# Gated convolution block with an 8x8 Fourier filter: the transform applied to the normalized channels before the projection

## The chip, the cores and the metric

One core of one Trainium2 chip runs the whole program. The metric is the device time of one execution in microseconds. TensorE is called PE here, VectorE DVE, ScalarE ACT, GpSimd POOL and SyncE SP, as in the profile.

## What is computed

The input x has 4 images of 32 channels with 128 by 128 pixels. Two layers follow one another; each adds a block of the normalized image to the image:

```python
xm = jnp.einsum('bchw,oc->bohw', x, W_in)                 # 32 -> 3*85 channels, x here normalized
x_spatial, x_freq, x_gate = jnp.split(xm, 3, axis=1)
out_spatial = jax.lax.conv_general_dilated(x_spatial, W_dw, ..., feature_group_count=HID)   # 3x3, per channel
xp = x_freq.reshape(B, HID, h, P, w, P).transpose(0, 1, 2, 4, 3, 5)                         # 8x8 patches
xf = jnp.fft.rfft2(xp)
xf = xf * fft_weight
xi = jnp.fft.irfft2(xf, s=(P, P))
x_fused = jax.nn.gelu(x_gate, approximate=False) * (out_spatial + out_freq)
return jnp.einsum('bchw,oc->bohw', x_fused, W_out)                                          # 85 -> 32
# x = x + block(gn(x)), twice; gn normalizes each channel of each image
```

The projection (over channels) and the Fourier transform (over the pixels of a patch) are both linear and act on different axes, so either can come first.

## The kernel before

The image is cut into Q = 4 bands of 32 columns, and the 128 partitions hold 4 bands x 32 channels. A strip is 8 columns wide in each band (4 strips for an image, 16 for a layer, 32 in all), a tile is 16 rows of a strip (two 8x8 patches, 128 pixels, for all 4 bands at once): 8 tiles to a strip, 256 tiles in both layers. Values are split into a high and a low f16 part (`parts`, HI and LO) and PE multiplies them in f16.

For each strip DVE normalizes into `xn` (L812), ACT rounds to the high part (L544, three shifts), DVE makes the low part (L836, three shifts), and SP copies `parts` into `stack`, where contraction rows are 4 groups of 32 channels (28 DMAs a strip, L273 and L279, two buffers; the buffer of strip s is free when the last tile of strip s-2 has ended, L284).

The main loop is written out by hand as steps, one for each tile, and every engine runs its own list in program order. Step i on PE, in this order: 7 convolution matmuls of tile i for band 0 (`conv`, L395, pixels stationary, 85 columns moving); 4 f32 transposes of the result of tile i-2 (L442); every fourth step, where i mod 4 is 2, the output projection of 4 tiles (L453); 2 gate matmuls and the convolution of band 1; the 4 frequency projections of tile i+3 into `ps_u` (L401); 2 gate matmuls, convolution of band 2; the Fourier transform of tile i+2, three matmuls of 340 columns (`bas` high and low against `uh`, high against `ul`, L482 to L485); convolution of band 3; the inverse transform of tile i, three matmuls of 340 columns (L490 to L493).

Beside it in step i: ACT copies `ft` (L579), rounds `uh` (L585), evaluates the gate's Gelu (L589), rounds `yh` (L594), and in steps 1, 3 and 5 of 8 makes the next strip's high parts. DVE multiplies by the gate (L895), adds the residual every fourth step (L905), in steps 0, 2, 4 and 6 of 8 normalizes and makes low parts, makes `ul` (L925), and multiplies the spectrum by its filter into `y32` (L931). POOL makes the low part `yl` of the filtered spectrum (L654), and seven times in the run sends and gathers statistics by DMAs of its own queue (L616, L622) and moves image edges (L634, L643). `y32`, `yh` and `yl` have two buffers each.

The order at the start is written out too: the first strip is split in two pieces, whose stack loads are shared by SP, POOL and ACT, and SP loads strip 1 after them.

## Time and profile before

| | us |
|---|---|
| median of 3 runs | 830.47 (828.88 to 832.42) |
| the profiled execution, its own time | 829.37 |
| its span | 827.6 |

| engine | busy us | share of the span |
|---|---|---|
| PE | 799.3 | 97% |
| DVE | 612.7 | 74% |
| ACT | 571.5 | 69% |
| POOL | 274.4 | 33% |

The profile is a page with busy shares, the chain of work that ended last and the costliest groups; the trace behind it answers by line, by stretch of time and by engine. A matmul's duration covers its way through the array and overlaps its neighbours': what it costs PE is the difference of the starts of two that follow one another. POOL's and SP's DMA rows are the time to issue; a DMA lands later, and its landing is counted from the start of its issue.

### The profile page before, as it was taken

What the parts mean: (1) busy time and instruction counts of PE and PEld (TensorE: products, weight loads), DVE (VectorE), ACT (ScalarE), POOL (GpSimd) and SP (SyncE); (2) the same over time, 40 slices, a digit from 0 to 9 for tenths busy, and PEclk for the clock granted to TensorE, in tenths of its full rate; (3) what the DMA queues carried; (4) which work ended last, traced back from release to release, by engine and by line L of the source; (5) the groups of instructions that cost most, each with busy time, mean ns of one, the idle gap of its engine ahead of it and who ended that gap; (6) DMA issues with size and microseconds to landing.
All of it is one profiled execution on the core that took longest, in us unless ns stands there. A gap on an engine that the chain in (4) does not pass through costs nothing.

```text
span 827.6 us, 31423 instructions
## 1 busy us (share of the span) xinstructions
PE 799.3 (97%) x12332; PEld 654.8 (79%) x12332; DVE 612.7 (74%) x1153; ACT 571.5 (69%) x1149; POOL 274.4 (33%) x345
## 2 busy tenths in 40 slices
PE   1799999999999999999999999999999999999997
PEld 0588888888888888888888888888888888888885
DVE  7887888888888777687777776667667766767553
ACT  2566676767767777777777777677776777777664
POOL 2724232542336322433234223332232333223221
PEclk9799999999999999999999999999999999999999
DMA  8766557545555445655454665655665655566621
GB/s 295 181 210 145 135 125 211 133 113 128 134 125 140 110 111 118 144 132 130 109 118 114 158 141 142 157 131 134 149 141 146 156 133 134 138 142 156 150 63 51
DMA packets 66522, 115.51 MB, mean 140 GB/s; under 512 B 16242, under 2 KB 18954, under 8 KB 65994
## 3 DMA queue, kind: packets, MB, share of 16 engines
q1 hardware_dynamic: 63606, 110.50, 54.1%
q0 software_dynamic: 2144, 2.59, 1.3%
q8 instruction: 99, 1.62, 0.9%
q10 hardware_dynamic: 628, 0.43, 0.2%
q14 instruction: 45, 0.37, 0.1%
HBM read 10.98 MB, written 8.56 MB: 24 GB/s over the span
## 4 chain that ended last, share of the span: by engine, by line
PE 94%; DVE 3%; issue 1%; DMA 1%; ACT 1%; SPq 0%; POOL 0%; DVEq 0%; ACTq 0%
PE ps_s L395 35%; PE ps_ft L442 15%; PE ps_o L453 8%; PE ps_g L401 6%; PE ps_u L401 5%; PE ps_z L482 5%; PE ps_s L490 5%; PE ps_s L493 4%; PE ps_s L491 4%; PE ps_z L485 4%; PE ps_z L483 4%; DMA x<-in_x 1%; DVE parts L836 1%; DVE st L755 0%; DVE amax L685 0%
## 5 line engine op out<-in xcount | busy, mean ns | idle before, releaser
L395 PE MATMUL ps_s<-cw,stack 128*128 128x85 f16 (+1 forms) x7168 | 457.5, 203 | 0.4 <-DVE f L895 0.4
L395 PEld LDWEIGHTS ps_s<-cw,stack 128*128 128x128 f16 (+1 forms) x7168 | 379.4, 98 | 49.1 <-DVE f L895 0.8
L654 POOL TENSOR_TENSOR yl<-y,yh 128x340 f16<-128x340 f32 x256 | 230.0, 899 | 525.4 <-ACT yh L594 525.4
L594 ACT ACTIVATE yh<-y 128x340 f16<-128x340 f32 x256 | 124.7, 487 | 195.6 <-DVE y L931 124.2
L925 DVE SCALAR_TENSOR_TENSOR ul<-ps_u,uh 128x340 f16<-128x340 f32 x256 | 129.7, 506 | 105.6 <-ACT uh L585 104.7
L836 DVE TENSOR_TENSOR parts<-xn,parts 128x1024 f16<-128x1024 f32 (+2 forms) x99 | 118.1, 1198 | 82.3 <-ACT parts L544 82.0
L579 ACT ACTIVATE ft<-ps_ft 85x512 f32<-85x512 f32 x256 | 149.3, 583 | 20.3 <-PE ps_ft L442 16.7
L442 PE MATMUL ps_ft<-squares_sb,f 128*85 128x128 f32 x1024 | 162.6, 281 | 0.8 <-ACT ft L579 0.8
L895 DVE TENSOR_TENSOR f<-ps_s,g 128x340 f32<-128x340 f32 x256 | 129.4, 505 | 12.5 <-PE ps_s L493 4.0
L589 ACT ACTIVATE g<-ps_g,gsc 128x340 f32<-128x340 f32 x256 | 137.6, 537 | 1.2 <-PE ps_g L401 1.0
L931 DVE TENSOR_TENSOR y<-ps_z,weff 128x340 f32<-128x340 f32 x256 | 128.2, 501 | 1.4 <-PE ps_z L485 1.4
L401 PE MATMUL ps_g<-pw,stack 128*128 128x85 f16 x1024 | 125.2, 205 | 0.0
L585 ACT ACTIVATE uh<-ps_u 128x340 f16<-128x340 f32 x256 | 114.5, 447 | 14.3 <-PE ps_u L401 13.2
L401 PEld LDWEIGHTS ps_g<-pw,stack 128*128 128x128 f16 x1024 | 80.2, 98 | 55.3 <-issue 52.8
L442 PEld LDWEIGHTS ps_ft<-squares_sb,f 128*85 128x85 f32 x1024 | 114.8, 155 | 1.0 <-DVE f L895 1.0
L544 ACT ACTIVATE parts<-xn 128x1024 f16<-128x1024 f32 (+2 forms) x99 | 100.3, 1017 | 15.4 <-DVE xn L820 14.2
L401 PE MATMUL ps_u<-pw,stack 128*128 128x85 f16 x1024 | 81.6, 202 | 1.1 <-DVE weff L732 1.1
L482 PE MATMUL ps_z<-uh,bas 128*128 128x340 f16 x256 | 79.2, 309 | 2.6 <-ACT uh L585 1.7
L490 PE MATMUL ps_s<-yh,inv 128*128 128x340 f16 x256 | 79.0, 309 | 0.0
L485 PE MATMUL ps_z<-ul,bas 128*128 128x340 f16 x256 | 78.7, 308 | 0.1
L493 PE MATMUL ps_s<-yl,inv 128*128 128x340 f16 x256 | 78.5, 307 | 0.0
L483 PE MATMUL ps_z<-uh,bas 128*128 128x340 f16 x256 | 78.5, 307 | 0.0
(96 smaller groups left out, 601.7 us busy)
## 6 DMA issues: line engine op xcount, KB each, us to landing
stack<-parts SPq DMA_DIRECT2D x496, 130.0 KB, 2.5
out_y<-yo SPq DMA_DIRECT2D x16, 512.0 KB, 2.8
stack<-parts SPq DMA_DIRECT2D x124, 65.0 KB, 2.1
stack<-parts SPq DMA_DIRECT2D x124, 64.5 KB, 2.1
stack<-parts SPq DMA_DIRECT2D x124, 64.0 KB, 2.0
x<-in_x SPq DMA_DIRECT2D x3, 2048.0 KB, 10.1
x<-in_x SPq DMA_DIRECT2D x4, 512.0 KB, 5.7
raw<-in_w_raw SPq DMA_DIRECT2D x2, 510.0 KB
```

Source lines behind the costliest of these rows:

```text
L395: mm(ps_s[i % 2][:, HID * q:HID * (q + 1)], pixels(kind, i, q, dy, rows), w[0:rows, m, :], start=(q == 0 and m == 0), stop=False)
L401: t = mm(bank[:, HID * q:HID * (q + 1)], pixels(A, i, q, 0), pw[layer(i)][:, which, :], start=(q == 0), stop=(q == Q - 1))
L442: t = nc.tensor.transpose(ps_ft[0:HID, q * 128:(q + 1) * 128], f[:, k, HID * q:HID * (q + 1)], id32)
L482: mm(ps_z[:, 0:GC], bas[:, 0, :], uh[:, k, :], start=True, stop=False)
L579: nc.scalar.activation(ft[:, (i - 2) % (2 * OUT), :, :].rearrange("p q n -> p (q n)"), ps_ft[0:HID, 0:Q * 128], ACT.Copy).then_inc(s_ft, 1)
L589: nc.scalar.activation(g[:, i % 2, :], ps_g[:, 0:GC], ACT.Gelu, scale=gsc[layer(i)][:, 0:1]).then_inc(s_gelu, 1)
L594: nc.scalar.activation(yh[:, i % 2, :], y32[:, i % 2, :], ACT.Copy).then_inc(s_yh, 1)
L654: nc.gpsimd.tensor_tensor(yl[:, k, :], y32[:, k, :], yh[:, k, :], ALU.subtract).then_inc(s_yl, 1)
L836: v.tensor_tensor(part[:, LO, rows], xn[:, rows, 1 + dx:1 + dx + TW], part[:, HI, rows], ALU.subtract).then_inc(s_xl, 1)
L895: v.tensor_tensor(f[:, k, :], ps_s[k][:, 0:GC], g[:, k, :], ALU.mult).then_inc(s_f, 1)
L925: v.scalar_tensor_tensor(ul[:, k, :], ps_u[k][:, 0:GC], US, uh[:, k, :], ALU.mult, ALU.subtract).then_inc(s_ul, 1)
L931: v.tensor_tensor(y32[:, k, :].rearrange("p (q o) -> p q o", q=Q), ps_z[:, 0:GC].rearrange("p (q o) -> p q o", q=Q), weff[layer(i + 2)][:, ...
```

## The change

The transform moves ahead of the projection. It is now applied to the 32 normalized channels: PE turns the pixels of two tiles (`turn`: the stored `parts`, channels by pixels, times an identity, 4 matmuls of 128 columns into `ps_xt`), ACT copies the turned pixels to `xt` (`turned_over`), PE transforms them one step later (`transform`: 3 matmuls of 128 columns for a tile), ACT and DVE split the spectra of four tiles into `xf` (`hi_of_spectrum`, `lo_of_spectrum`), and POOL's queue copies them into `xs`, where three groups of 32 channels lie on 96 partitions (high, high, low): 12 DMAs of 32 partitions x 512 f16 for four tiles, three in each step, ahead of that step's `yl` in POOL's order. PE then forms `ps_z` by 4 matmuls of 85 columns. `ps_u`, `uh` and `ul` go, and so do the three transform matmuls of 340 columns. The turn of a pair of tiles stands 12 steps before the pair's first tile, the split of a group of four 8 steps before its first tile, its DMAs 6 to 3 steps before, and PE uses it from 2 steps before. The start is reordered and carries the spectra of the first eight tiles; its matmuls that only keep PE busy are split up. Piece 1 of the first strip is loaded by SP and POOL alone. PE waits for both kinds of stack loads at the strip's first convolution, no longer for one kind three steps ahead. Some buffers share memory.

```diff
@@ -38,11 +38,17 @@
 SS = XS * WS
 EPS = 1e-5
 HI, LO = 0, 1
-LEAD = 3
+LEAD = 2
 DRAIN = 4
-WARM = 32
+
+WARM = (6, 4, 8, 4, 6)
 
 OUT = 4
+
+PAIR, GROUP = 2, 4
+PAIRS, GROUPS_OF_TILES = TILES // PAIR, TILES // GROUP
+
+SPECTRA = (0, 0, 1)
 KH = P * (P // 2 + 1)
 
 
...
 THIRDS = [(k, q) for q in range(Q) for k in range(3)]
 
 PIECES = ((0, 72), (72, H))
-FIRST_LOADS = [(PAIRS_HI[0::2], PAIRS_LO[0::2], THIRDS[0::3]), (PAIRS_HI[1::2], PAIRS_LO[1::2], THIRDS[1::3]),
-               ([], [], THIRDS[2::3])]
+FIRST_LOADS = [[(PAIRS_HI[0::2], PAIRS_LO[0::2], THIRDS[0::3]), (PAIRS_HI[1::2], PAIRS_LO[1::2], THIRDS[1::3]),
+                ([], [], THIRDS[2::3])],
+               [(PAIRS_HI[i::2], PAIRS_LO[i::2], THIRDS[i::2]) for i in range(2)]]
 
 
 STATS = [(0, 0), (0, 1), (1, 0), (0, 2), (1, 1), (0, 3), (1, 2), (1, 3)]
...
+
+        xt = sb("xt", [128, PAIR, 2, 128], F16)
+        xf = sb("xf", [128, 2, 2, GROUP * 128], F16)
+        xs = sb("xs", [3 * C, 2, Q, GROUP * 128], F16)
         g = sb("g", [128, 2, GC])
         y32 = sb("y32", [128, 2, GC])
...
@@ -307,12 +325,37 @@
                 for load in hi:
                     if load[0] == k:
                         load_pair(eng, 0, load, loaded[0], a, z)
+            if piece == 0:
+                for q in range(Q):
+                    load_spectrum(eng, 0, q, s_xs_first[0][by], (by,))
             eng.wait_ge(s_xl, before + ORDER.index(1) + 1)
             for load in lo:
                 load_pair(eng, 0, load, loaded[0], a, z)
             eng.wait_ge(s_xl, before + ORDER.index(-1) + 1)
             for load in thirds:
                 load_third(eng, 0, load, loaded[1], a - 2 * TW if a else 0, z - 2 * TW if z < SC else SC)
+
+
+        def turns_at(p):
+            return PAIR * p - 12 if p >= 8 else p - 4
+
+        def leaves_at(h):
+            return turns_at(2 * h + 1) + 2
+
+        def loads_at(h, q):
+            return 4 * h - 6 + q if h > 2 else (3, 3, 4, 4)[q]
+
+        turning = {turns_at(p): p for p in range(4, PAIRS)}
+        transforming = {turns_at(p) + 1: p for p in range(4, PAIRS)}
+        leaving = {leaves_at(h): h for h in range(2, GROUPS_OF_TILES)}
+
+        def load_spectrum(eng, h, q, loaded, rows=range(3)):
+
+            need(eng, s_z, GROUP * (h - 1))
+            for k in rows:
+                eng.wait_ge((s_xfh, s_xfl)[SPECTRA[k]], h + 1)
+                eng.dma_start(xs[C * k:C * k + C, h % 2, q, :],
+                              xf[C * q:C * q + C, h % 2, SPECTRA[k], :]).then_inc(loaded, 16)
 
         def store(sp, strip):
 
@@ -341,6 +384,8 @@
             load_image(1)
             for piece in range(len(PIECES)):
                 load_piece(sp, piece, 0)
+            for q in (0, 1):
+                load_spectrum(sp, 1, q, s_xs_first[1][0])
             for strip in range(1, ALL):
                 load_strip(sp, strip)
...
+            def turn(p):
+
+                strip = PAIR * p // TPS
+                pe.wait_ge(s_xl, (1 if p < 2 else 1 + len(ORDER)) if strip == 0 else splits(strip, 0))
+                need(pe, s_xt, p)
+                for j in range(PAIR):
+                    at = TW + PIX * ((PAIR * p + j) % TPS)
+                    for part in (HI, LO):
+                        col = 128 * (2 * j + part)
+                        m = mm(ps_xt[:, col:col + 128], parts[strip % 2][:, part, 1, at:at + PIX], id16[:, :],
+                               start=True, stop=True)
+                m.then_inc(s_xt_made, 1)
+
+            def transform(p):
+
+                pe.wait_ge(s_xt, p + 1)
+                if p % 2 == 0:
+                    need(pe, s_xfh, p // 2)
+                    need(pe, s_xfl, p // 2)
+                for j in range(PAIR):
+                    out = ps_x[:, 128 * ((PAIR * p + j) % GROUP):128 * ((PAIR * p + j) % GROUP) + 128]
+                    mm(out, xt[:, j, HI, :], bas[:, 0, :], start=True, stop=False)
+                    mm(out, xt[:, j, HI, :], bas[:, 1, :], start=False, stop=False)
+                    m = mm(out, xt[:, j, LO, :], bas[:, 0, :], start=False, stop=True)
+                m.then_inc(s_dft, 1)
+
+            for p in range(4):
+                turn(p)
+                warm(WARM[p])
+                transform(p)
+            warm(WARM[4])
 
...
+            def spectra_loaded(h):
+                if h == 0:
+                    for by in range(3):
+                        pe.wait_ge(s_xs_first[0][by], 16 * Q)
+                elif h == 1:
+                    for by in range(2):
+                        pe.wait_ge(s_xs_first[1][by], 16 * 2 * 3)
+                else:
+                    pe.wait_ge(s_xs[h % 2], 16 * 3 * Q * (h // 2))
...
-                    project(ps_g, 1, i, range(Q // 2))
+                    gate(i, range(Q // 2))
                     if i > 0:
                         conv(i, 1)
-                if live(i, 3):
-                    if begins(i + 3):
-                        stacks_loaded(i + 3, 0)
-                    if (i + 3) % LT == 0:
-                        pe.wait_ge(s_projection, PROJECTIONS * (layer(i + 3) + 1))
-                        pe.wait_ge(s_weff, layer(i + 3) + 1)
-                    need(pe, s_uh, i + 2)
-                    need(pe, s_ul, i + 2)
-                    project(ps_u[(i + 3) % 2], 0, i + 3, range(Q)).then_inc(s_u, 1)
+                if i in turning:
+                    turn(turning[i])
                 if live(i, 0):
-                    project(ps_g, 1, i, range(Q // 2, Q)).then_inc(s_gate, 1)
+                    gate(i, range(Q // 2, Q)).then_inc(s_gate, 1)
                     conv(i, 2)
                 if live(i, 2):
-                    k = i % 2
-                    need(pe, s_uh, i + 3)
+                    if (i + 2) % LT == 0:
+                        pe.wait_ge(s_projection, PROJECTIONS * (layer(i + 2) + 1))
+                        pe.wait_ge(s_weff, layer(i + 2) + 1)
+                    if (i + 2) % GROUP == 0:
+                        spectra_loaded((i + 2) // GROUP)
                     need(pe, s_y, i + 2)
-                    mm(ps_z[:, 0:GC], bas[:, 0, :], uh[:, k, :], start=True, stop=False)
-                    mm(ps_z[:, 0:GC], bas[:, 1, :], uh[:, k, :], start=False, stop=False)
-                    need(pe, s_ul, i + 3)
-                    mm(ps_z[:, 0:GC], bas[:, 0, :], ul[:, k, :], start=False, stop=True).then_inc(s_z, 1)
+                    col = 128 * ((i + 2) % GROUP)
+                    for q in range(Q):
+                        z = mm(ps_z[:, HID * q:HID * (q + 1)], xs[:, (i + 2) // GROUP % 2, q, col:col + 128],
+                               pw[layer(i + 2)][0:3 * C, 0, :], start=(q == 0), stop=(q == Q - 1))
+                    z.then_inc(s_z, 1)
+                if i in transforming:
+                    transform(transforming[i])
                 if live(i, 0):
                     conv(i, 3)
...
+            def turned_over(p):
+
+                act.wait_ge(s_xt_made, p + 1)
+                need(act, s_dft, p)
+                nc.scalar.activation(xt[:, :, :, :].rearrange("p a b n -> p (a b n)"), ps_xt[:, :],
+                                     ACT.Copy).then_inc(s_xt, 1)
+
+            def hi_of_spectrum(h):
+                act.wait_ge(s_dft, 2 * h + 2)
+
+                need(act, s_z, GROUP * (h - 2) + 1)
+                nc.scalar.activation(xf[:, h % 2, 0, :], ps_x[:, :], ACT.Copy, scale=US).then_inc(s_xfh, 1)
+
...
             load_piece(act, 0, 2)
-            load_piece(act, 1, 2)
...
+                if i in leaving:
+                    hi_of_spectrum(leaving[i])
-                if live(i, 3):
-                    k = (i + 3) % 2
-                    need(act, s_u, i + 4)
-                    need(act, s_z, i + 2)
-                    nc.scalar.activation(uh[:, k, :], ps_u[k][:, 0:GC], ACT.Copy, scale=US).then_inc(s_uh, 1)
+                if i in turning:
+                    turned_over(turning[i])
...
             for i in steps():
+                if i in (-1, 0):
+                    load_spectrum(pool, 1, i + 3, s_xs_first[1][1])
+                for h in range((i + 3) // GROUP, (i + 6) // GROUP + 1):
+                    for q in range(Q):
+                        if 2 <= h < GROUPS_OF_TILES and loads_at(h, q) == i:
+                            load_spectrum(pool, h, q, s_xs[h % 2])
...
+                                       ALU.mult, ALU.subtract).then_inc(s_xfl, 1)
 
             v.memset(table[:, :], 0.0).then_inc(s_table, 1)
             v.memset(ones[:, :], 1.0)
...
-                if live(i, 3):
-                    k = (i + 3) % 2
-                    need(dve, s_uh, i + 4)
-                    need(dve, s_z, i + 2)
-                    v.scalar_tensor_tensor(ul[:, k, :], ps_u[k][:, 0:GC], US, uh[:, k, :],
-                                           ALU.mult, ALU.subtract).then_inc(s_ul, 1)
...
+                if i in leaving:
+                    lo_of_spectrum(leaving[i])
```

`bas` and `inv` keep their contents; `id16` is the 128 by 128 identity in f16.

## Rows read from the trace of the kernel before

**Rows 1.** The page: busy time of PE, and its granted clock in 40 slices.

```profile
PE 799.3 (97%) x12332; PEld 654.8 (79%) x12332; DVE 612.7 (74%) x1153; ACT 571.5 (69%) x1149; POOL 274.4 (33%) x345
PEclk9799999999999999999999999999999999999999
```

**Rows 2.** One line of the kernel, L493, the last matmul of a step.

```profile
L493 PE MATMUL ps_s<-yl,inv x256: 306/306/489, 37.6 to 819.8; 128*128 128x340 f16 x128
```

**Rows 3.** Timeline, PE, from step 2 of a strip: start us, us, line, xcount.

```profile
507.69 0.45 PE L395 MATMUL ps_s<-cw,stack 128*128 128x85 f16 x7
507.97 0.63 PE L442 MATMUL ps_ft<-squares_sb,f 128*85 128x128 f32 x4
...
509.91 0.32 PE L401 MATMUL ps_u<-pw,stack 128*128 128x85 f16 x4
510.07 0.24 PE L401 MATMUL ps_g<-pw,stack 128*128 128x85 f16 x2
...
510.43 0.31 PE L482 MATMUL ps_z<-uh,bas 128*128 128x340 f16 x1
...
510.87 0.45 PE L395 MATMUL ps_s<-cw,stack 128*128 128x85 f16 x7
...
511.58 0.45 PE L395 MATMUL ps_s<-cw,stack 128*128 128x85 f16 x7
...
514.38 0.45 PE L395 MATMUL ps_s<-cw,stack 128*128 128x85 f16 x7
```

**Rows 4.** Groups by line: xcount, busy us, mean ns of one, idle before.

```profile
L579 ACT ACTIVATE ft<-ps_ft 85x512 f32<-85x512 f32 x256 | 149.3, 583 | 20.3 <-PE ps_ft L442 16.7
L925 DVE SCALAR_TENSOR_TENSOR ul<-ps_u,uh 128x340 f16<-128x340 f32 x256 | 129.7, 506 | 105.6 <-ACT uh L585 104.7
L905 DVE SCALAR_TENSOR_TENSOR yo<-ps_o,osc,x 128x512 f32<-128x512 f32 x32 | 23.7, 742 | 3.1 <-PE ps_o L453 3.1
```

**Rows 5.** Timeline, POOL, ACT and DVE, around steps 4 and 5 of the strip.

```profile
515.27 0.83 POOL L654 TENSOR_TENSOR yl<-y,yh 128x340 f16<-128x340 f32 x1 [1.96 <-ACT yh L594]
518.90 0.83 POOL L654 TENSOR_TENSOR yl<-y,yh 128x340 f16<-128x340 f32 x1 [2.80 <-ACT yh L594]
...
515.03 1.04 ACT L544 ACTIVATE parts<-xn 128x1024 f16<-128x1024 f32 x1
518.27 0.49 ACT L594 ACTIVATE yh<-y 128x340 f16<-128x340 f32 x1 [0.95 <-DVE y L931]
...
516.17 1.23 DVE L836 TENSOR_TENSOR parts<-xn,parts 128x1024 f16<-128x1024 f32 x1 [1.09 <-ACT parts L544]
```

**Rows 6.** Lines L279, L622 and L643, POOL's DMAs: ns, then us to landing.

```profile
L279 POOL DMA_DIRECT2D stack<-parts x8: 496/500/515, 21.9 to 29.9; - x8
DMA to landing us min/median/max: 2.6/3.4/4.3
...
L622 POOL DMA_DIRECT2D gathered<-sums x28: 548/552/597, 68.8 to 450.0; - x28
...
DMA to landing us min/median/max: 1.9/2.3/4.0
...
DMA to landing us min/median/max: 1.7/2.1/3.9
```

**Rows 7.** Timeline, DVE and POOL, where a normalization meets `yl` in step 0.

```profile
502.73 0.94 DVE L812 TENSOR_SCALAR xn<-x,mv,rstd 128x1280 f32<-128x1280 f32 x1
502.99 1.38 POOL L654 TENSOR_TENSOR yl<-y,yh 128x340 f16<-128x340 f32 x1 [1.86 <-ACT yh L594]
```

**Rows 8.** Timeline, SP's queue and PE: strip 1 at the start, a later strip.

```profile
44.64 7.87 SPq L279 DMA_DIRECT2D stack<-parts  x12
...
60.23 0.45 PE L395 MATMUL ps_s<-cw,stack 128*128 128x85 f16 x7
...
379.57 11.68 SPq L273 DMA_DIRECT2D stack<-parts  x16
391.31 8.47 SPq L279 DMA_DIRECT2D stack<-parts  x12
```

More of the change, by code:

```diff
@@ L211, in build @@
                    for i in range(len(PIECES))]
-        s_u = sem("s_u")
-        s_uh = sem("s_uh")
-        s_ul = sem("s_ul")
+        s_id16 = sem("s_id16")
+        s_xt_made = sem("s_xt_made")
+        s_xt = sem("s_xt")
+        s_dft = sem("s_dft")
+        s_xfh = sem("s_xfh")
+        s_xfl = sem("s_xfl")
+        s_xs_first = [[sem(f"s_xs_first_{by}_{h}") for by in ("sp", "pool", "act")] for h in range(2)]
+        s_xs = [sem(f"s_xs{i}") for i in range(2)]
         s_z = sem("s_z")
@@ L250, in staged @@
         def staged(i, parts_of_a_strip):
-            if i < 0:
-                at = 2 * (i + LEAD)
-                return 1, [p for p in parts_of_a_strip.values() if at <= p < at + 2 or i == -1 and p > at]
             strip, at = i // TPS + 2, i % TPS
@@ L296, in load_strip, with count @@
                 load_third(eng, strip, load, s_stk[strip % 2][1])
+        def count(loads, kind):
+            return 16 * (len(loads[0] + loads[1]), len(loads[2]))[kind]
         def load_piece(eng, piece, by):
-            (hi, lo, thirds), loaded = FIRST_LOADS[by], s_first[piece][by]
+            (hi, lo, thirds), loaded = FIRST_LOADS[piece][by], s_first[piece][by]
             first, last = PIECES[piece]
@@ L396, in conv, with gate @@
                        start=(q == 0 and m == 0), stop=False)
-            def project(bank, which, i, bands):
+            def gate(i, bands):
                 for q in bands:
-                    t = mm(bank[:, HID * q:HID * (q + 1)], pixels(A, i, q, 0), pw[layer(i)][:, which, :],
+                    t = mm(ps_g[:, HID * q:HID * (q + 1)], pixels(A, i, q, 0), pw[layer(i)][:, 1, :],
                            start=(q == 0), stop=(q == Q - 1))
                 return t
+            def spectra_loaded(h):
[7 more added lines that the diff above has]
+                    pe.wait_ge(s_xs[h % 2], 16 * 3 * Q * (h // 2))
             def stacks_loaded(tile, kind):
-                def count(loads):
-                    return 16 * (len(loads[0] + loads[1]), len(loads[2]))[kind]
                 strip = tile // TPS
                 if strip == 0:
-                    for by, loads in enumerate(FIRST_LOADS):
-                        need(pe, s_first[tile // (TPS // 2)][by][kind], count(loads))
+                    for by, loads in enumerate(FIRST_LOADS[tile // (TPS // 2)]):
+                        need(pe, s_first[tile // (TPS // 2)][by][kind], count(loads, kind))
                 else:
-                    pe.wait_ge(s_stk[strip % 2][kind], (strip + 1) // 2 * count((PAIRS_HI, PAIRS_LO, THIRDS)))
+                    pe.wait_ge(s_stk[strip % 2][kind], (strip + 1) // 2 * count((PAIRS_HI, PAIRS_LO, THIRDS), kind))
             def begins(tile):
@@ L422, in conv_begins @@
                 if begins(i):
+                    stacks_loaded(i, 0)
                     stacks_loaded(i, 1)
@@ L552, in hi_part @@
                     need(act, s_s, (strip - 2) * TPS + 1)
+                    if strip == 2:
+                        for by, loads in enumerate(FIRST_LOADS[1]):
+                            for kind in range(2):
+                                act.wait_ge(s_first[1][by][kind], count(loads, kind))
                 hi(strip, dx, slice(0, H))
-            def hi_piece(piece):
-                act.wait_ge(s_xn, 2 * piece + 2)
-                for dx in ORDER:
-                    hi(0, dx, slice(*PIECES[piece]))
             act.wait_ge(s_table, 1)
@@ L737, in first_taps @@
                 dve.wait_ge(s_vl, 1)
-                for kind in (A, BB):
-                    for k in range(4):
-                        _, dx, part = GROUPS[k][kind]
-                        v.tensor_copy(cw[0][C * k:C * k + C, 3 * kind:3 * kind + 3, :],
-                                      (vh, vl)[part][C * k:C * k + C, dx + 1::3, :]).then_inc(s_taps, 1)
+                for part, groups in ((vh, slice(0, 3 * C)), (vl, slice(C, 2 * C))):
+                    last = v.tensor_copy(cw[0][groups, 0:6, :].rearrange("p (k t) o -> p k t o", k=2),
+                                         part[groups, :, :].rearrange("p (t d) o -> p d t o", d=3)[:, 1:3, :, :])
+                    if part is vh:
+                        link(last)
+                last.then_inc(s_taps, 6)
             def image_stats(b, n):
```

103 lines of the change are left out of this document (66 added, 37 removed).

## The prediction

> **What bounds the kernel now.** I read the page's busy shares first: PE 97%, no other engine above 74%, at a granted clock of 9 tenths or more in all slices but one [rows 1]. That makes PE the candidate, and the rest is asked of it. The last matmul of a step stands at 37.6 us for the first tile and at 819.8 for the last [rows 2]: 782.2 us for 255 steps, 3.067 each, 24.5 for a strip of eight. The timeline of one strip, read by differences of starts, says what fills them: a plain step takes 2.80 us (511.58 to 514.38) and the step with the output projection 3.89 (507.69 to 511.58), so four take 3 x 2.79 + 3.89 = 12.27, which is 4 x 3.067: every step of the run is like these, PE is never late, and a matmul removed is time removed as long as nothing takes its place. Seven convolution matmuls of 85 columns cost 0.28, 40 ns each; the four frequency projections 510.07 - 509.91 = 0.16; the three transform matmuls of 340 columns 510.87 - 510.43 = 0.44, 147 ns each [rows 3].
>
> **PE's own sum.** Removed for a tile: 0.16 + 0.44 = 0.60 us. Added: four matmuls of 85 columns for `ps_z`, 4 x 0.040 = 0.16; two of 128 columns to turn, three of 128 to transform. No row shows an f16 matmul of 128 columns. Scaled by columns from 340 it is 0.147 x 128 / 340 = 55 ns, from 85 it is 0.040 x 128 / 85 = 61; its bounds are the 40 of an 85-column one below and the 147 of a 340-column one above. I take 55, since the larger size carries less of the cost of starting: 5 x 0.055 = 0.275. Added 0.435, net 0.60 - 0.435 = 0.165 us a tile, 0.66 for four. With 61 it is 0.135. After the start 248 steps are left: 248 x 0.165 = 40.9 us (33.5 with 61 ns).
>
> A new even step is then 2.79 - 0.60 + 0.16 + 0.22 (the turn of two tiles) = 2.57 and an odd one 2.79 - 0.60 + 0.16 + 0.33 (their transform) = 2.68, the one with the projection 3.67; a strip is 23.2.
>
> **DVE and ACT.** DVE loses `ul`, 0.51 a tile, and gains the low part of four tiles' spectra; the nearest row is 512 elements out of PSUM, 0.74, or 0.19 a tile. ACT loses `uh`, by columns 0.58 x 340 / 512 = 0.39 a tile or a little more, and gains a copy of 512 elements for two tiles and one for four, at 0.58 each: 0.44 [rows 4]. Both had room for this (74% and 69%), so these cost nothing by themselves, covered by PE; without the cover ACT's order counts, in step 4 of a strip (below).
>
> **POOL.** It gains three DMA issues in each step, ahead of `yl`. The nearest row for one of 32 partitions x 1 KB is its own stack load, 0.50; a gather takes 0.55 [rows 6]. 3 x 0.50 + 0.83 = 2.33 us of a mean step of 2.90: it fits, in the time in which POOL waited for `yh` (1.96 and 2.80 us in the rows) [rows 5]. What is queued behind the issues is `yl`, for which the filtering of two tiles later and the inverse transform wait, some 3 us after its usual end. The gathers (4 x 0.55, seven times) may use that up: under 1 us each, in the range, not in the sum.
>
> **The new wait, where I expect part of the gain to go.** PE's `ps_z` of the first tile of a group, in a step whose number is 2 mod 4, waits for DMAs of which the last three are issued in the step before. Call T the start of a step. `yl` starts 515.27 - 514.38 = 0.89 after T [rows 3, 5]. In step 1 of a strip: in step 0 `yl` meets the normalization and takes 1.38 [rows 7], to T0 + 2.26; three issues end at T0 + 3.8, which is T1 + 1.2, the next `yl` at 2.06, and the third issue after it starts at T1 + 3.1. PE wants `ps_z` in step 2 at 2.74 - 0.16 + 0.22 = 2.80, which is T1 + 5.48: 2.4 us are allowed for the landing. In step 5: step 3's high part on ACT (515.03 before) now has the split of a spectrum, the copy of `ft`, the Gelu and the turned pixels behind it before the next `yh`, some 0.95 + 4 x 0.47 after 515.03; that is 517.9 where it was 518.27 (there it waited for `y32` behind the low part of 516.17 and `ul`), `yl` follows 0.63 later and ends at 519.3, in the new count T5 + 2.4; the third issue starts at T5 + 3.4 and 2.1 are allowed. Against this the landings from start of issue: gathers 1.9 / 2.3 / 4.0, edges 1.7 / 2.1 / 3.9, stack loads in the crowded start 2.6 / 3.4 / 4.3 (least, median, most) [rows 6]. The gathers are nearest (24 KB, at the same steps of a strip, while SP loads a stack), so 2.3: step 1's groups are in time and step 5's 0.2 late; the long landings add, by my estimate, 0.17 to either. Mean 0.27 us for each of 62 groups, 17 us. Bounds: 0 with 1.9, and 1.2 us, 74 in all, with 3.4.
>
> **The start.** SP is busy with stack loads without a gap; strip 1's last issue ends at 44.64 + 7.87 = 52.5, lands 2.1 later by the edges' median, and step 8 starts at 60.2, so 5.6 us of slack [rows 6, 8]. SP gains 4 issues for the first spectra, 2 more thirds and 6 for the second: 12 x 7.87 / 12 = 7.9 us, past the slack by 2.3. I put 2.3 us there, between -1 and 4; the earlier first steps are worth nothing, as PE then stands before step 8.
>
> **SP afterwards.** A strip's 28 issues take 11.68 + 8.47 = 20.2 us, with the landing 22.3 [rows 8], of 24.5 before and 23.2 now. Cost nothing, with about 0.9 us of cover.
>
> **Sum.** 829.4 (profiled run, its span 827.6 and 1.8 around it) + 2.3 - 40.9 + 17 = 807.8. The median before stands 1.1 above its profiled run: 809.
>
> **Rivals.**
> 1. The spectra land in time and the gain comes whole: 829.4 + 2.3 - 40.9 + 1.1 = 792. For it, the least landings; against it, that step 5 allows only 2.1.
> 2. Slower: the landings of the last three spectrum DMAs are as in the start, 3.4 us. Then each group waits 1.2 us: 792 + 74 = 866. It decides at (40.9 - 2.3) / 62 = 0.62 us late for each group, a landing of some 2.85. For it, the rows of the same kind of transfer, SBUF to SBUF beside SP's loads; against it, that those were queued behind each other.
> 3. Just around that point, 0.55 to 0.8 us late: 826 to 842.
> 4. SP's loads of a strip, now beside 14% more traffic (384 packets of 1 KB in four tiles), stretch from 20.2 to 23, and with the landing outlast the 23.2: 2 us for each of 31 strips, 62 in all, 854 at worst, 823 if it is half of that. Against it: the issues set the pace, not the landings.
> 5. The 128-column matmul costs about 80 ns, between the 61 and the 147: 0.60 - 0.16 - 0.40 = 0.04 a tile, 10 us in all, and with the wait of the forecast 829.4 + 2.3 - 10 + 17 + 1.1 = 840; as steps are longer then, the wait shrinks, 823 to 840. Against it: weights are loaded for each 85-column matmul within its 40 ns. The Trainium skill states such a price (TensorE: Matmul & The Clock Gate, Back-to-back issue gap): a sustained stream at 128 columns with a weight load each runs at about 81 ns a matmul. The trace doesn't agree in its neighbourhood (40 ns at 85 columns, 147 at 340), and so this has a small chance.
> 6. POOL's DMA issue is held while a normalization runs. `yl` is: 1.38 us in place of 0.83 beside L812, once a strip [rows 7]. If the three issues after it lose as much, step 1's groups are 0.5 later, 31 x 0.5 = 16 us: 825. The Trainium skill has this rule (SBUF — State Buffer, Who interferes with whom): a DMA of GpSimd's queue needs that engine to write descriptors over the port pair that VectorE's two-port modes lock, and SP's or ACT's queue should be used instead. The trace agrees for `yl`; no POOL DMA here met a normalization in the loop.
>
> **How the numbers follow.** Forecast (0.1 to 0.45 us late, 797 to 819, rival 6's milder half in it) 0.45; rival 1, 0.20; rival 6 in full and rival 3 together, 0.12 (a third of it faster, half the same, the rest slower); rival 2, 0.10; rival 4, 0.07 (half same, half slower); rival 5, 0.06 (half faster, a third the same). The band of 0.5% is about what a measurement can tell from no change, 826.3 to 834.6. Faster 0.45 + 0.20 + 0.04 + 0.03 = 0.72; same 0.06 + 0.03 + 0.02 = 0.11; slower 0.17. Range: from 788 (rival 1 with 53 ns) to 836; above it lie rival 2 and the worst of 3, 4 and 5, about 0.17. Within the forecast itself 797 to 819.
>
> **What would show it.** Right: differences of starts of 0.22 for `turn`, 0.33 for `transform`, 0.16 for `ps_z`; PE idle before `ps_z` in steps 2 mod 4 alone, released by DMA into `xs`, longer in steps 6 than in steps 2 of a strip; POOL's issues at 0.50 and its busy time near 650 us; steps 2.57 and 2.68; step 8 starting near 62. Wrong: idle of PE before `ps_s` for `yl` (then POOL is too full), before the first convolution of a strip (then SP), a step of four longer than 11.6 without idle (then the matmul's price), or POOL issues over 0.6 us.

## The result, and the profile after

The changed kernel takes 874.97 us (median of 4 runs, 872.05 to 879.0) against 829.67 for the one before (4 runs beside it): 1.054 times as long, interval 1.049 to 1.060. The forecast was 809, its range 788 to 836, so it is wrong in sign and outside its range. The profiled execution took 879.0 us, its span 877.2: 49.6 us more than the profiled run of before.

The page of the changed kernel: busy times, the clock granted to PE in 40 slices, the chain that ended last, and three of its groups (line, operation, xcount, busy us, mean ns, idle before and its releaser). They answer to [rows 1, 4].

```profile
PE 790.4 (90%) x12840; PEld 672.1 (77%) x12840; DVE 559.1 (64%) x956; ACT 573.0 (65%) x1087; POOL 643.5 (73%) x1101
...
PEclk9698999899999999999999989999999999899999
...
PE 47%; POOL 19%; DMA 15%; issue 8%; ACT 6%; DVE 3%; ACTq 1%; POOLq 0%; SPq 0%; DVEq 0%
...
L357 POOL DMA_DIRECT2D xs<-xf x754 | 377.2, 505 | 11.9 <-issue 9.5
...
L567 PE MATMUL ps_z<-pw,xs 96*128 96x85 f16 x1024 | 83.4, 206 | 51.1 <-DMA xs<-xf 50.6
...
L654 ACT ACTIVATE xt<-ps_xt 128x512 f16<-128x512 f32 x128 | 75.4, 589 | 8.6 <-issue 4.8
```

PE has lost its 97%: it is busy for 9 us less and stands still. One wait is new and large, the one before `ps_z` for the spectra. The chain, which before was PE's, now runs through POOL and the DMAs.

The first question is whether PE's own work became shorter, as planned. The timeline of an undisturbed odd and an even step (start us, us, line, xcount) answers to [rows 3]:

```profile
560.57 0.45 PE L474 MATMUL ps_s<-cw,stack 128*128 128x85 f16 x7
...
562.05 0.31 PE L567 MATMUL ps_z<-pw,xs 96*128 96x85 f16 x4
562.20 0.22 PE L454 MATMUL ps_x<-bas,xt 128*128 128x128 f16 x1
...
562.54 0.45 PE L474 MATMUL ps_s<-cw,stack 128*128 128x85 f16 x7
...
563.25 0.45 PE L474 MATMUL ps_s<-cw,stack 128*128 128x85 f16 x7
...
564.38 0.39 PE L442 MATMUL ps_xt<-id,parts 128*128 128x128 f16 x4
564.60 0.24 PE L480 MATMUL ps_g<-pw,stack 128*128 128x85 f16 x2
...
565.84 0.45 PE L474 MATMUL ps_s<-cw,stack 128*128 128x85 f16 x7
```

Differences of starts: the odd step 563.25 - 560.57 = 2.68, the even one 2.59, the transform of two tiles 562.54 - 562.20 = 0.34, the turn 0.22, `ps_z` 0.15. These are the forecast's 2.68, 2.57, 0.33, 0.22 and 0.16. A strip without a wait takes 23.3 us by these steps (24.53 before); experiment 3 shows it. Where no turn or transform is left, in the last 12 steps, a plain step takes 2.36. Together that is the 41 us that PE's sum promised.

So 829.4 - 41 = 788, and 91 us came on top. The last matmul of each of the 256 steps, first and last of them (it answers to [rows 2]), and the first convolution of step 8:

```profile
L579 PE MATMUL ps_s<-yl,inv x256: 306/306/492, 43.2 to 869.4; 128*128 128x340 f16 x128
...
69.90 0.45 PE L474 MATMUL ps_s<-cw,stack 128*128 128x85 f16 x7 [1.01 <-DVE f L1024]
```

Step 8 starts at 69.90 where it was 60.23 [rows 8]: 9.7 us. Read from the starts of these matmuls, the 31 groups whose `ps_z` stands in step 2 of a strip are late by 51 us together (1.64 each), the 31 in step 6 by 12 (0.39 each). The other steps take 18 us more than their length, 16 of them the steps right behind ten of these waits. 788 + 9.7 + 63 + 18 = 879.

**Where the wait comes from.** All landings of POOL's spectrum DMAs, then those of the last three DMAs of two groups of one strip, issued in its step 1 and in its step 5, and the share of the 16 DMA engines over that strip (576 to 600 us in 40 slices):

```profile
L357 POOL DMA_DIRECT2D xs<-xf x754: 496/498/1091, 23.1 to 853.8; - x189
...
DMA to landing us min/median/max: 1.7/2.3/9.2
```

```profile
L357 POOL DMA_DIRECT2D xs<-xf x3: 496/496/512, 580.4 to 581.4; - x3
...
DMA to landing us min/median/max: 3.0/3.1/3.1
...
L357 POOL DMA_DIRECT2D xs<-xf x3: 496/496/512, 593.0 to 594.0; - x3
...
DMA to landing us min/median/max: 1.9/1.9/2.0
```

```profile
DMA  4263659989899887965979965540445674656697
```

The median of all, 2.3, is just what I had assumed, and it misleads. A landing depends on the step of the strip in which the DMA is issued: by median 2.0, 2.9, 3.0, 2.5, 2.1, 2.0, 1.9 and 1.7 us in steps 0 to 7. Steps 1 to 3 are those in which SP's large pair loads are under way (the nines of the last row). Step 1 had been given the longer allowance, 2.4 us, and needs 3.2 for the last DMA of its group.

The 51 us of the step 2 groups divide so, by issue and landing of each group's last DMA. Twenty-one groups issued on time (by median 2.9 us after the start of step 1) wait 13.6 us together. Four behind a gather of statistics (last issue 4.4 to 5.8 after it) wait 15.6. Two beside a 2 MB image load (landings 8.4 and 6.0) wait 10.9. Two wait 5.6, where POOL stood 2.15 and 1.94 us in the midst of the group's issues with nothing to wait for that the trace shows, and two, issued 3.7 after it behind an edge copy, wait 5.0. So a quarter of the 51 us is the usual landing, and three quarters are rare events. The step 6 groups are as forecast: last issue 3.3 us after the start of step 5, landing 2.2.

**The clock behind a wait.** Timeline and stretches of the group behind a gather (columns of the stretches: busy us and count by engine, PE's granted clock, DMA share, GB/s):

```profile
505.65 1.53 POOL L357 DMA_DIRECT2D xs<-xf  x3
508.12 0.47 PE L567 MATMUL ps_z<-pw,xs 96*128 96x85 f16 x4 [3.94 <-DMA xs<-xf]
508.39 0.71 PE L474 MATMUL ps_s<-cw,stack 128*128 128x85 f16 x7
```

```profile
499.00:503.20 4.20, 4.20 (x65) 3.05 (x64) 3.19 (x7) 3.20 (x6) 4.17 (x8) 1.00 0.92 231
504.40:508.10 3.70, 0.00 (x0) 0.00 (x0) 0.00 (x0) 0.57 (x2) 2.78 (x5) 0.81 0.84 222
508.10:512.40 4.30, 4.28 (x43) 3.81 (x44) 2.02 (x5) 1.28 (x3) 1.72 (x3) 0.50 0.57 156
```

Before the wait POOL is busy for 4.17 of 4.20 us: it works off the gather's backlog, and the group's loads leave late. In the wait PE does nothing, and its granted clock falls from 1.00 to a mean of 0.81. After it PE runs for some 4 us at a granted clock of 0.50, the lower of its two levels (1.2 GHz of 2.4); seven convolutions show 0.71 us instead of 0.45. Short waits mostly have no such price: the 21 groups issued on time are late by at most 1.9 us, and the steps behind all of them together take 0.1 us more than their length; the ten others are late by 2.2 to 6.8 us, and the steps behind them take 16 more. Between the two it goes either way: PE stands idle 1.7 us before `ps_z` in step 50 and as long in step 58, and only in step 50 does its granted clock fall to 0.50. (Of the 51 us, 4 are slow matmuls too: `ps_z` itself starts 47 us late in these steps, the rest follows it within the step.)

**The start.** The queues of ACT and SP:

```profile
24.44 2.52 ACTq L357 DMA_DIRECT2D xs<-xf  x4
27.06 2.50 ACTq L293 DMA_DIRECT2D stack<-parts  x4
29.66 0.60 ACT L654 ACTIVATE xt<-ps_xt 128x512 f16<-128x512 f32 x1 [4.78 <-issue]
...
26.71 2.50 SPq L293 DMA_DIRECT2D stack<-parts  x4
33.14 6.00 SPq L287 DMA_DIRECT2D stack<-parts  x8
```

ACT issues eight DMAs from 24.4 to 29.6, and its high parts of piece 1 stand behind them (32.5); SP, which needs these, idles from 29.2 to 33.1. The forecast had counted SP's added issues and taken SP to stay busy.

### The profile page after: what moved, and what is told of

Same layout as the page of the kernel before. It is cut to its first block, busy times and chain, and to the rows that moved or that the text cites. A ratio compares the mean times of both kernels' runs of the same rounds, so it can differ in the third digit from the quotient of the medians.

```text
span 877.2 us, 32629 instructions
## 1 busy us (share of the span) xinstructions
PE 790.4 (90%) x12840; PEld 672.1 (77%) x12840; DVE 559.1 (64%) x956; ACT 573.0 (65%) x1087; POOL 643.5 (73%) x1101
## 4 chain that ended last, share of the span: by engine, by line
PE 47%; POOL 19%; DMA 15%; issue 8%; ACT 6%; DVE 3%; ACTq 1%; POOLq 0%; SPq 0%; DVEq 0%
PE ps_s L474 18%; DMA xs<-xf 14%; POOL xs L357 9%; POOL yl L772 8%; PE ps_ft L529 7%; PE ps_z L567 4%; PE ps_s L576 3%; PE ps_s L579 3%; PE ps_s L577 3%; PE ps_g L480 3%; PE ps_o L540 3%; ACT yh L703 2%; ACT turned_results L691 1%; PE ps_xt L442 1%; ACT xt L654 1%
## 5 line engine op out<-in xcount | busy, mean ns | idle before, releaser
L357 POOL DMA_DIRECT2D xs<-xf x754 | 377.2, 505 | 11.9 <-issue 9.5
L955 DVE TENSOR_TENSOR parts<-xn,parts 128x1024 f16<-128x1024 f32 (+2 forms) x99 | 124.7, 1261 | 93.9 <-ACT parts L630 93.7
L529 PE MATMUL ps_ft<-squares_sb,f 128*85 128x128 f32 x1024 | 167.5, 287 | 0.8 <-ACT turned_results L691 0.8
L691 ACT ACTIVATE turned_results<-ps_ft 85x512 f32<-85x512 f32 x256 | 149.4, 584 | 28.5 <-PE ps_ft L529 28.2
L567 PE MATMUL ps_z<-pw,xs 96*128 96x85 f16 x1024 | 83.4, 206 | 51.1 <-DMA xs<-xf 50.6
L529 PEld LDWEIGHTS ps_ft<-squares_sb,f 128*85 128x85 f32 x1024 | 118.7, 159 | 1.0 <-DVE f L1024 1.0
L567 PEld LDWEIGHTS ps_z<-pw,xs 96*128 96x128 f16 x1024 | 55.3, 100 | 57.7 <-DMA xs<-xf 56.5
L654 ACT ACTIVATE xt<-ps_xt 128x512 f16<-128x512 f32 x128 | 75.4, 589 | 8.6 <-issue 4.8
L576 PE MATMUL ps_s<-yh,inv 128*128 128x340 f16 x256 | 80.9, 316 | 0.0
L577 PE MATMUL ps_s<-yh,inv 128*128 128x340 f16 x256 | 80.0, 313 | 0.0
L540 PE MATMUL ps_o<-turned_results,wo 85*32 85x512 f32 x512 | 68.2, 605 | 0.7 <-ACT turned_results L691 0.7
```

The lines of the kernel that those rows point to most:

```text
L357: eng.dma_start(xs[C * k:C * k + C, h % 2, q, :], xf[C * q:C * q + C, h % 2, SPECTRA[k], :]).then_inc(loaded, 16)
L529: t = nc.tensor.transpose(ps_ft[0:HID, q * 128:(q + 1) * 128], f[:, k, HID * q:HID * (q + 1)], id32)
L567: z = mm(ps_z[:, HID * q:HID * (q + 1)], xs[:, (i + 2) // GROUP % 2, q, col:col + 128], pw[layer(i + 2)][0:3 * C, 0, :], start=(q == 0), s ...
L691: nc.scalar.activation(ft[:, (i - 2) % (2 * OUT), :, :].rearrange("p q n -> p (q n)"), ps_ft[0:HID, 0:Q * 128], ACT.Copy).then_inc(s_ft, 1)
L955: v.tensor_tensor(part[:, LO, rows], xn[:, rows, 1 + dx:1 + dx + TW], part[:, HI, rows], ALU.subtract).then_inc(s_xl, 1)
```

## Experiments

The theory after the result, A: PE's saving is real, and the loss is lateness of the spectra, which makes the transfers' time before `ps_z` the only thing to repair. The rival, B: the work that the change adds (754 issues on POOL, traffic beside SP's loads, POOL's time) slows other things, and would do so if nobody waited for the spectra.

**1. The loads a step earlier.**

```diff
-            return 4 * h - 6 + q if h > 2 else (3, 3, 4, 4)[q]
+            return 4 * h - 7 + q if h > 2 else (3, 3, 4, 4)[q]
```

> The changed kernel with POOL's spectrum loads one step earlier (steps 7 to 4 before a group's first tile in place of 6 to 3), nothing else moved. Theory A, late landing: what the change lost in its loop is PE's wait for these DMAs before ps_z (63 us in the profile of after, in steps 2 and 6 of a strip) and the halved clock behind the long ones (14 us). A step is 2.7 us, and only waits longer than that are left, some 11 us: 875 - 52 - 11 = about 812. Theory B, crowding: the 12% of DMA time and the 377 us of POOL's issues slow the rest wherever they stand: 870 to 880.

Measured 824.11 us (5 runs, 821.19 to 827.18), 0.993 of before (0.990 to 0.996): 51 us less than the change as made, by one number. The waits of this kernel (us, times, longest):

```profile
PE ps_z L567 <- DMA xs<-xf: 12.0, 8, 3.0
```

A holds in direction; its 812 was missed by 12.

**2. The spectra not read.** The loads are issued as before, but `ps_z` multiplies a constant in place of `xs`, so the Fourier branch of the result is left out, and PE doesn't wait for them in the loop. ACT and POOL wait instead, before they use a buffer again, until the loads out of it have landed; that costs ACT 1.4 us and PE nothing that its waits show.

```diff
-                    z = mm(ps_z[:, HID * q:HID * (q + 1)], xs[:, (i + 2) // GROUP % 2, q, col:col + 128],
+                    z = mm(ps_z[:, HID * q:HID * (q + 1)], bas[0:3 * C, 0, :],
```

> The changed kernel, but from tile 8 on ps_z is formed from the constant basis and not from the spectra: the result is not the reference's. All loads are still issued at their places and land, PE waits for none. Theory A: the loop runs at its own steps, 2.58, 2.69 and 3.68 us: about 797 (start as in after, to 72.3; 29 strips of 23.27; the rest 50). Theory B: 840 or more.

Measured 817.69 us (2 runs). Neither 797 nor 840: 57 us of the loss is the wait for the spectra with its consequences, and some 15 to 20 (this run against experiment 3 and against the 797 expected) is B's. The waits name it:

```profile
PE ps_s L579 <- POOL yl L776: 10.8, 7, 3.2
```

In the strips with gathers POOL is a step behind, and `yl` is late as well.

**3. No loads in the loop.** As 2, with POOL's issues in the loop left out too.

```diff
-                            load_spectrum(pool, h, q, s_xs[h % 2])
+                            pass
```

> As the run whose spectra are not read, and POOL's spectrum loads of the loop left out too (the result is not the reference's; turn, transform and splits are all still done). Theory A: the same as that run within 4 us, about 797 or a little less, since issues and traffic by themselves cost nothing. Theory B: under 800 here and 40 us or more between the two runs.

Measured 802.18 us (2 runs), 0.966 of before. From strip 2 to the last but two a strip takes 23.3 us, but for two of 23.8 and 23.5; strip 1 takes 25.9. The run lies 15.5 below experiment 2, not within 4 as A had it: the loads cost that much even where nobody reads them. Issues and transfers went out together here, so their shares aren't separated; the 10.8 us for `yl` in experiment 2 point to the issues. It is the floor for anything done to the loads alone: PE's 41 us are there, the start's 9.7 are not repaired.

**4. The kernel before, with the loads.** Three DMAs of 32 partitions x 1 KB in each step, from a table that lies ready, which nobody reads and nobody waits for.

```diff
+                if 2 <= i < 246:
+                    q = (i - 2) % 4
+                    need(pool, s_spare[q], 16 * 3 * ((i - 2) // 4))
+                    for k in range(3):
+                        pool.dma_start(ft_all[96:128, ...], squares_sb[C * q:C * q + C, :, :]...).then_inc(s_spare[q], 16)
```

> The kernel before, with three extra DMAs of 32 partitions x 1 KB issued by POOL ahead of yl in each of steps 2 to 245, from a constant into memory nobody reads: the change's traffic and issues alone. Theory A: 830 within 3 us, with SP's landings longer but nobody late. Theory B: 850 to 875.

Measured 838.84 us (2 runs), 1.010 of before (1.006 to 1.015). Its line and one wait that it has and before has not:

```profile
L657 POOL DMA_DIRECT2D ft<-squares_sb x732: 496/498/1092, 43.5 to 799.3; - x183
...
DMA to landing us min/median/max: 1.7/2.5/9.0
...
PE ps_u L403 <- DMA stack<-parts: 3.6, 2, 2.4
```

This kernel measures what was disputed, the landing, without the change: by median 2.3, 2.7, 3.1, 3.0, 2.3, 2.0, 2.0 and 1.7 us for issues in steps 0 to 7 of a strip, the same course, with 9.0 at worst beside an image load. So the long landings don't come from how `xf` is made. In both kernels they fall in the steps of SP's pair loads (0.87 to 1.01 of the DMA engines' time in steps 1 to 3, 0.2 to 0.3 in step 7); that these loads are the cause is inferred from this, as no run moved or left out the burst. The loads by themselves cost 9 us here, in the steps beside gathers and image loads (step 37, beside image 3's, takes 5.39 instead of 2.79).

**5. The gathers on ACT's queue.** Sends, gathers and edges move from POOL's list to ACT's, the four gathers of a lot spread over three steps, the rest as changed.

```diff
+            def gather(e, q):
+                act.wait_ge(s_sent, 16 * e)
+                act.wait_ge(s_mv, e)
+                act.dma_start(gathered[C * q:C * q + C, :, :], sums[e].rearrange("(q c) n -> c q n", q=Q)).then_inc(s_gathered, 16)
```

> The changed kernel with the statistics' sends and gathers and the edge transfers issued by ACT's queue (gathers spread over three steps) in place of POOL's, which leaves POOL the spectrum loads, yl and small work; the loads stand where the change has them. If POOL's backlog after a gather is what made the last loads late by 4 to 6 us in the groups of steps 42, 74, 106 and 138 (15.6 us of wait there, and 7 of slow clock behind it), those are gone and the landing beside the pair loads stays: 875 - 20 = 855, within 8. If the backlog matters little: 870 or more. If ACT becomes late by it: PE would idle before its gate matmuls.

Measured 866.09 us (2 runs).

```profile
PE ps_z L567 <- DMA xs<-xf: 49.4, 42, 5.0
```

In the groups of step 2 the late issues are gone (last issue 2.9 by median, 3.7 at most, and the mean falls from 1.64 to 1.34 us late), but the groups of step 6 rose from 0.39 to 0.63. Of the 20 us expected 9 came. What took the rest stands in POOL's timeline:

```profile
201.32 0.50 POOL L357 DMA_DIRECT2D xs<-xf  x1 [2.49 <-issue]
...
325.33 0.50 POOL L357 DMA_DIRECT2D xs<-xf  x1 [2.50 <-issue]
```

Six times POOL stands 2.5 us before a DMA issue with no releaser in the trace, exactly 120 of its DMAs apart, and each time in step 5, among the last loads of the group of step 46, 86, 126, 166, 206 or 246. These six steps take 8.9 us more than their length.

**6. Both.** Experiments 1 and 5 together.

> Both: spectrum loads a step earlier, and sends, gathers and edges by ACT. The run with early loads alone was at 824, with PE still waiting in the strips with a gather (steps 10, 42, 74, 106, 138) and where an image is loaded. Theory A with the backlog: some 15 us less, 808 to 812. If the rest is due to traffic alone: 822 to 826.

Measured 814.92 us (4 runs, 812.81 to 817.15), 0.982 of before (0.979 to 0.985): 9 less than experiment 1, with the ranges apart. POOL's six pauses are there as in experiment 5, but the earlier loads cover them: the steps behind them are at their length.

```profile
PE ps_z L567 <- DMA xs<-xf: 4.7, 2, 2.8
```

```profile
L357 POOL DMA_DIRECT2D xs<-xf x7: 496/496/514, 149.8 to 159.5; - x7
...
DMA to landing us min/median/max: 5.6/7.6/7.9
```

From step 48 on the strips are at 23.3 to 24.1 us up to the last steps, which are so short that PE waits 2.1 for the last strip's stack. The rest of what is left sits beside the image loads: the second fence is the stretch of image 3's, where spectra land after 5.6 to 7.9 us.

**7. A pause of PE, by itself.** In the kernel before, PE waits in step 2 of 31 strips for twelve memsets of POOL.

```diff
+                if i % TPS == 2 and 10 <= i < TILES:
+                    pool.wait_ge(s_s, i)
+                    for n in range(PAUSE):
+                        nc.gpsimd.memset(spare[:, :], 0.0).then_inc(s_pause, 1)
...
+                    if i % TPS == 2 and i >= 10:
+                        pe.wait_ge(s_pause, PAUSE * (i // TPS))
```

> The kernel before, with PE waiting before ps_z in step 2 of each strip from step 10 on (31 times) for 12 chained memsets of POOL, no other change. It measures what an idle time of about 3 us costs beyond itself. If the granted clock falls behind such a wait, as the profile of after shows behind waits over 2 us, 830 + 31 x (the wait + 1 to 2 us); if that was an effect of the traffic, 830 + 31 x the wait, and the next steps stay at 2.79.

Measured 1027.66 us (2 runs), span 1024.9, 197.3 more than before.

```profile
PE ps_z L487 <- POOL spare L658: 114.6, 31, 6.7
```

```profile
416.00:419.00 3.00, 2.81 (x21) 2.04 (x22) 0.92 (x2) 0.35 (x1) 0.05 (x1) 0.50 0.54 125
...
422.00:424.00 2.00, 2.00 (x36) 1.80 (x34) 1.02 (x2) 0.98 (x2) 0.35 (x1) 1.00 0.43 100
```

The waits make 114.6 us, 3.7 each; the other 82.7, 2.7 for each wait, lie behind them, where PE works at a granted clock of 0.50 (2.81 us busy for 21 matmuls) until it is back at 1.00. A wait of 3.7 us costs 6.4. The forecast's sum had priced a microsecond late at a microsecond.

**8. The order of the start.** ACT makes the high parts of piece 1 before its eight DMA issues, DVE the low parts before the loop.

```diff
+            hi(0, ORDER[1], slice(*PIECES[1]))
+            hi(0, ORDER[2], slice(*PIECES[1]))
             load_piece(act, 0, 2)
             turned_over(2)
```

> The changed kernel with one edit in the start: ACT makes the high parts of piece 1 before its 8 DMA issues (which hold it for 5.1 us) and DVE its low parts before the loop. SP was idle from 29.2 to 33.1 us waiting for them and its loads of strip 1 set when step 8 starts (68.7 against 60.2 before). Expected: step 8 about 4 us earlier, total 871 within 3. If the first steps are bound by the turn and its copies instead: 875 again.

```profile
29.20 5.15 SPq L287 DMA_DIRECT2D stack<-parts  x8
...
66.68 0.45 PE L474 MATMUL ps_s<-cw,stack 128*128 128x85 f16 x7
...
PE ps_z L567 <- DMA xs<-xf: 60.2, 46, 5.5
```

SP's piece 1 leaves at 29.20 instead of 33.14 and step 8 starts at 66.68 instead of 69.90. Yet it measures 881.5 us (2 runs, 879.86 to 883.14), 6.5 more than the change as made: the waits before `ps_z` are 60.2 us here against 50.6. Why they grew, this run doesn't tell.

**9. Image loads in quarters.** Experiment 6, with images 2 and 3 loaded by four DMAs of 0.5 MB each, image 2's one behind the stack loads of strip 1 and three between those of strip 2, image 3's one for a strip.

```diff
-                    load_image(2)
-                if strip == 4:
-                    load_image(3)
+                    quarter(2, 0)
+                if strip in (3, 4, 5, 6):
+                    quarter(3, strip - 3)
```

> The kernel of e6 (POOL's loads of the spectra a step earlier, gathers, sends and edges issued by ACT), in which the loads of images 2 and 3, 2 MB each, are four loads of 0.5 MB: image 2's in the strip loads of strips 1 and 2, image 3's one behind each of the strip loads 3 to 6. What is left of e6 over its own nominal strip are steps 9, 10 and 11 (+5.3 us together) and steps 33 and 34 (+4.4 us), both beside an image load. Theory A (a 2 MB load keeps the 16 engines for some 6 us, and spectra issued meanwhile land after 7 to 9 us): steps 33 and 34 back to 2.69 and 3.7, steps 9 to 11 back by half or more, 807 to 809 us. Rival B (the same bytes cost the same time wherever they stand, spread over more steps): 813 to 816.

Measured 810.79 us (4 runs), 0.977 of before (0.975 to 0.979). Steps 34 and 35, which the text on record counts as 33 and 34, are back at their length (3.68 and 2.69 from 7.28 and 3.54), as A had it. Image 2 went wrong: steps 14 and 15 take 7.33 and 6.79.

```profile
DVE mv L932 <- DMA gathered<-sums: 8.5, 1, 8.5
```

Three quarters between the pair loads hold everything behind them (median landings of 8 to 11 us by kind of DMA, the gathers among them), and DVE waits for these in its order with the filter and the gate behind it.

**10. With the order of the start.**

> The kernel of e9, and the order of e8 in the start: ACT's high parts of piece 1 before its own eight DMA issues, DVE's low parts of that piece before the loop. In e8 step 8 began 3 us earlier (65.8 against 68.7) and the waits before ps_z ate it. Theory A (those waits were late spectra, which the earlier loads have removed): the 3 us stay, 804 to 806 us. Rival B (the early strips are held by SP's loads of the first strips, whose order is not changed): within 1 us of e9.

Measured 808.19 us (4 runs, 803.89 to 812.62), 0.973 of before (0.970 to 0.976). Steps 10 and 11 are undisturbed now, 14 and 15 (7.62 and 6.75; its next text counts them as 13 and 14) are not. The runs of 9 and 10 overlap, so the gain of the start isn't shown by their medians. (Its text puts step 8 of two kernels at 65.8 and 68.7; the first convolutions stand at 66.68 and 69.90.)

**11. Image 2 behind strip 2.** Experiment 10, with the last three quarters of image 2 behind strip 2's stack loads.

```diff
+                if strip == 2:
+                    for n in (1, 2, 3):
+                        quarter(2, n)
```

> The kernel of e10, with three of the four quarters of image 2 behind the strip loads of strip 2 instead of between them. In e9 and e10 steps 13 and 14 take 8.8 and 8.1 us longer than their nominal 6.4, because the gathers of image 1's sums, issued behind the quarters, land after 10 to 11 us and DVE stands 8.5 us before its mean and variance. Theory A (the place, not the bytes): those two steps come back to nominal, one group of spectra behind the quarters is late by up to 3 us, 801 to 804 us. Rival B (1.5 MB more in the queue hold strip 3 or the gathers as much): 808 or more.

Measured 804.66 us (5 runs, 804.36 to 806.63), 0.971 of before (0.970 to 0.972).

```profile
PE ps_z L575 <- DMA xs<-xf: 2.1, 1, 2.1
...
L587 PE MATMUL ps_s<-yl,inv x256: 306/306/492, 42.3 to 794.5; 128*128 128x340 f16 x128
```

Strip 1 is at its length (23.38 us), one group, in step 18, is late by 2.3 us behind the quarters, and the strips after it take 23.3 to 24.6. It comes within 3 us of experiment 3, in which no spectrum is loaded in the loop (though that one has the start as changed), and it beats the kernel before by 25 us. A is carried for the larger part. B has a share too: the gathers and the loads together were too much for POOL, and moving the gathers was worth 9 us (experiment 6 against 1).

## Why the prediction was wrong

The forecast's 809 and the profiled 879.0 lie 70 us apart. The term that failed is the wait before `ps_z`: 17 us in the sum, 63 measured, with 18 behind it for which the sum had no term; the start adds 7.4. (These make 71; the forecast already held 1 for the distance of median and profiled run.) Of the 46 us that were missing in the wait 8 are the usual landing in step 1 (13.6 instead of 5.3), 21 the issues behind gathers and edge copies, 11 the image loads and 6 POOL's own pauses.

- **PE's own sum: right.** 128-column matmuls stand 55 to 57 ns apart (0.34 for six), in runs of four and six with a weight load each. The Trainium skill states about 81 for a sustained stream of this kind (TensorE: Matmul & The Clock Gate, Back-to-back issue gap); the trace doesn't agree. Rival 5 is out. (The range's lower end, "rival 1 with 53 ns", comes to 789 by its own terms and not 788.)
- **POOL's price: right.** 0.50 us an issue, 643.5 us busy (650 forecast), and `yl` hardly late for PE by itself.
- **The step 5 groups: right.** Allowed 2.1, last issue 3.3 (3.4 forecast), 0.39 us late by mean (0.37).
- **The step 1 groups: the landing mis-sized.** The landing was taken from the gathers, 2.3 [rows 6], one median over two phases. Of the 28 gathers, read one by one with their step, the 12 in steps 2 and 3 of a strip land after 2.2 to 3.7 us, median 2.7, the 16 in steps 6 and 7 after 1.9 to 4.0, median 2.2; the rows below show one lot of each. So the trace of before had the phases, and the 2.2 of the quiet one is what step 5's groups then took. In step 1 the last landing is 3.2 by median, near the crowded start's 3.4, the row that I had put aside. Nor does a group wait for a median: it waits for its last DMA, and in each of the three lots of steps 2 and 3 the last gather landed slowest, after 3.7, 3.2 and 2.9 us. 5 us of these groups' lateness were forecast, 51 measured, and they wait longer than the step 5 groups, not shorter. Twenty-one of the 31 lose 13.6 us to that landing alone; the two points below have most of the rest. The gathers of the kernel before, a lot issued in steps 2 and 3 and one in steps 6 and 7:

```profile
L622 POOL DMA_DIRECT2D gathered<-sums x4: 548/552/597, 166.4 to 168.0; - x4
...
DMA to landing us min/median/max: 2.2/2.6/3.2
...
L622 POOL DMA_DIRECT2D gathered<-sums x4: 548/552/561, 350.5 to 352.1; - x4
...
DMA to landing us min/median/max: 1.9/2.0/2.1
```

- **The gathers: the step that cost most, left out of the sum.** "Under 1 us each" held one backlog by itself; but the backlog meets the new loads, which meet PE's wait: 3.0 to 4.7 us for each of four groups, and 2.2 and 2.9 for two behind edge copies.
- **The image loads: not thought of.** Two waits of 6.8 and 4.1 us. In the kernel before no step beside them is more than 0.1 us longer than another, since PE needed none of what was issued there so soon.
- **The clock behind waits: left out.** 16 us here, 2.7 for a wait of 3.7 in experiment 7.
- **The start: 2.3 forecast, 9.7 measured.** SP's added issues were counted, but ACT's were not followed to who waits for them: SP's queue stood 3.9 us, and step 8 still a microsecond for DVE behind.
- **Rival 2** had the mechanism, a landing of 3.4 us, and gave 866. It reached 875's neighbourhood partly by chance: only 12 of the 62 last landings take 3.4 us or more, and backlog, images, clock and start make the rest. **Rival 4** is out in this form: no wait of PE for the stacks of a strip is among the large ones, though the pair loads land after 3.4 us instead of 2.5 and the bytes moved rose by 22% (140.8 MB from 115.5), not by the 14% it had. **Rival 1**'s time, with the start as it is, is experiment 3.
- **Rival 6.** Six of the 754 issues took 0.68 to 1.09 us instead of 0.50, each while DVE normalized; the median of all that overlapped a normalization is 0.51. That is 2 us in all. The Trainium skill's rule cited there (SBUF — State Buffer, Who interferes with whom) may show at those six, and it decides nothing.

## What to carry to other kernels

Before a copy is put between a producer and the engine that sets the time, take its landing from the phase of the loop in which it will be issued, beside whatever burst runs then, and not from a median or from a transfer of like size in another phase. Then look for the rare events that share its queue or the DMA engines (statistics, an image), and price a long wait of PE at more than its length. A lead of one step more was worth 51 us here, and it cost nothing, since the buffers allowed it.

## What the runs showed that I had not expected

- The landing of one and the same DMA (32 partitions x 1 KB, POOL's queue) has medians from 1.7 to 3.1 us by its place in a strip, in two different kernels; beside a load of 2 MB it is 5.6 to 9.2. Each such load is one DMA to issue and delays those that come after it, on SP's, POOL's and ACT's queues (a send of ACT's took 9.4 beside image 2 in experiment 6).
- A wait of PE of 3.7 us is followed by work at the lower clock that costs 2.7 more; in the changed kernel groups late by up to 1.9 us had nothing behind them.
- POOL stood four times for 1.9 to 2.2 us before or between its DMA issues with no releaser in the trace (in the page's "issue 9.5"); experiment 4 has 9.1 us of it in six places. It comes with the number of POOL's DMAs and not with time: in experiments 5, 6, 9, 10 and 11 there are six such pauses of 2.0 to 2.5 us, exactly 120 of its DMAs apart, which is every 126 us in experiment 5 and every 117 in experiment 6. Experiment 3 and the kernel before, with few such DMAs, have none. Why is open.
